# A gated-triangle mix stage in slots of four tiles instead of two, with fewer and wider norm chains

## The reference, cut to what matters

```
zn  = layernorm(layernorm(x)) * ln_g + ln_b               # x, and three pair inputs alike
ab  = sigmoid(zn @ Wg + bg) * (zn @ W + b)                # three gated projections, 64 channels
blk = einsum(pp, ab1) + einsum(ab2, lp) + ab3 * ip        # the triangle: 192 x 192 x 64
g   = sigmoid(zn @ Wend + bend)
x2  = x + g * (layernorm(blk) * lnc_g + lnc_b) @ Wsum ... * z_mask     # the mix stage
t   = layernorm(x2)
logits = mean over all positions of t, per channel, @ Wr + br          # routing: 2 of 8 experts
out = t-stream + ffn(t)                                                # the feed-forward stage
```

## Time and profile before

| | |
|---|---|
| median of three runs | 1568.2 us |
| the profiled execution's own time | 1569.81 us |
| its span | 1568.1 us |
| mean granted TensorE clock | 0.955 |
| busy share of the span | PE 88%, DVE 78%, POOL 64%, ACT 63% |
| DMA, mean over the span | 172 GB/s |

### The profile page before, as it was taken

One profiled execution on the slowest core, in us unless ns is written; L12 is line 12 of the kernel. 1 busy time (PEld: TensorE's weight loads), 2 busy tenths in 40 slices (PEclk: granted clock), 3 DMA queues, 4 the chain that ended last, 5 costly groups with the idle time before them and its releaser, 6 DMA issues. The chain is left out here.

```text
span 1568.1 us, 33771 instructions
## 1 busy us (share of the span) xinstructions
PE 1383.9 (88%) x9869; PEld 1152.2 (73%) x9869; DVE 1223.8 (78%) x4389; ACT 986.0 (63%) x2295; POOL 1007.0 (64%) x1547
## 2 busy tenths in 40 slices
PE   5999999999999996878778999779999999999992
PEld 2877777877777775767556666569898888999882
DVE  6898888888888973645479999757888888888874
ACT  3877777778778783322236777434676666766762
POOL 3888888888889884433337888533555555555553
PEclk9999999999999998989889999979999999999996
DMA  9989899989899978767678999311222222222212
GB/s 211 240 218 240 224 238 243 230 224 232 225 244 226 241 193 236 219 175 244 173 195 262 297 299 297 117 51 41 68 77 73 67 80 80 68 79 80 69 41 80
DMA packets 358354, 270.34 MB, mean 172 GB/s; under 512 B 60710, under 2 KB 333054, under 8 KB 358206
## 3 DMA queue, kind: packets, MB, share of 16 engines
q1 hardware_dynamic: 356924, 268.16, 63.7%
q10 hardware_dynamic: 1010, 0.20, 0.1%
q0 software_dynamic: 272, 0.21, 0.1%
HBM read 174.16 MB, written 94.37 MB: 171 GB/s over the span
## 5 line engine op out<-in xcount | busy, mean ns | idle before, releaser
L1466 ACT ACTIVATE hT<-psH_d,b 128x512 f32<-128x512 f32 x288 | 197.8, 689 | 171.4 <-PE psH_d L1506 171.3
L1491 PE MATMUL psY_d<-w,hT 128*128 128x128 f32 x2304 | 268.9, 275 | 0.0
L1491 PEld LDWEIGHTS psY_d<-w,hT 128*128 128x128 f32 x2304 | 262.9, 192 | 0.1
L639 PE MATMUL psZ_a<-w_all,xT_a 128*128 128x128 f32 x1728 | 239.1, 283 | 23.4 <-ACT xT_a L549 23.4
L639 PEld LDWEIGHTS psZ_a<-w_all,xT_a 128*128 128x128 f32 x1728 | 216.6, 197 | 30.8 <-ACT xT_a L549 28.4
L639 PE MATMUL psZ_a<-w_all,xT_block 128*128 128x384 f32 x576 | 213.3, 493 | 9.2 <-DVE ab_a L710 9.2
L565 ACT ACTIVATE sig_a<-psZ_a 128x256 f32<-128x256 f32 (+1 forms) x360 | 153.8, 427 | 93.3 <-PE psZ_a L639 53.5
L1524 POOL TENSOR_TENSOR u_d<-u_d,gamma 128x512 f32<-128x512 f32 x72 | 95.9, 1331 | 159.9 <-ACT u_d L1452 142.3
L626 PE MATMUL psT_a<-ident,shared 128*128 128x128 f32 x1152 | 189.3, 278 | 4.7 <-issue 3.3
L626 PEld LDWEIGHTS psT_a<-ident,shared 128*128 128x128 f32 x1152 | 143.8, 144 | 55.9 <-issue 28.0
L577 POOL TENSOR_SCALAR shared<-shared,coefs_ix 128x128 f32<-128x128 f32 x348 | 154.9, 456 | 39.6 <-DVE coefs_ix L360 37.4
(11 more groups left out here) (219 smaller groups left out, 3023.7 us busy)
## 6 DMA issues: line engine op xcount, KB each, us to landing
shared<-in_x_dram SPq DMA_DIRECT2D x48, 512.0 KB, 5.6
scratch_xT<-xT_block SPq DMA_DIRECT2D x36, 512.0 KB, 4.9
shared<-scratch_xT SPq DMA_DIRECT2D x36, 512.0 KB, 4.8
scratch_x<-x_c SPq DMA_DIRECT2D x36, 512.0 KB, 4.0
shared<-scratch_x SPq DMA_DIRECT2D x36, 512.0 KB, 3.6
shared<-in_x_dram SPq DMA_DIRECT2D x48, 256.0 KB, 5.1
shared<-L_conv_protein_pair_dram SPq DMA_DIRECT2D x24, 512.0 KB, 7.3
shared<-in_L_conv_l_pair_dram SPq DMA_DIRECT2D x24, 512.0 KB, 6.2
```

The costliest lines, as they stand in the source:

```text
L639: ins = nc.tensor.matmul(out, turned_x(G, i, t0, size)[:, j * P:j * P + P], rhs[i], start=True, stop=True)
L1466: nc.scalar.activation(hT[:, g % 2, f, :], psH[:, f, :], ACT.Gelu, bias=s["b1"][:, f:f + 1]).then_inc(gelued, 1)
L1491: ins = nc.tensor.matmul(psY[:, g % 2, i * CH:i * CH + CH], hT[:, g % 2, f, i * P:i * P + P], s["w2"][:, f, :], start=(f == 0), stop=(f == ...
```

## The change: what it does

- A slot is four tiles (a quad): 72 slots instead of 144 pairs. In a slot ACT normalises tiles 0 and 2 and POOL tiles 1 and 3, two slots ahead, into three buffers; PE makes two transposes, four psZ and two psW matmuls; the copy, gate, y and add work on 256, 512, 512 and 512 elements a row.
- Chains no longer follow the blocks. Ten chains (`CHAINS_C`): chains 0 to 2 for the triangle's quads 0 to 5, 6 to 11 and 12 to 20, chains 3 to 6 for 12, 12, 12 and 15 quads of the triangle together with 12 quads of x2 each, chains 7 to 9 for the last x2 quads. A chain has 18 steps; the last one makes the scale, shift and copy in up to three operations. Chains 1 and 2 have two slots (nine steps each), chains 3 to 8 three slots (six each), chain 0 and 9 stand alone. In a slot DVE interleaves: step, y, (triangle tiles); then four times step, one x2 tile, (triangle tiles); then any further steps.
- The triangle's tiles are measured ahead as `MEASURED` says: 12 a slot in slots 0 and 1, 6 in slots 2 to 7, 9 or 10 in 8 to 12, 4 in 13 to 36, 5 in 37 to 48, none after.
- x2 has three block buffers; route of a quad follows `ROUTED_IN`: one quad a slot from slot 17, two a slot from slot 65, three in 71 and 72, the last six after the last chain.
- `coef_t` is one buffer for all tiles, and x2's coefficients are used from the buffer that the FFN stage reads.

```diff
+QUADS = TPB // 4
+SLOTS_C = QUADS * NBLK
+X2_RING = 3
+TRI_GROUPS = ((0, 6), (6, 12), (12, 21), (21, 33), (33, 45), (45, 57), (57, 72))
+X2_GROUPS = ((0, 12), (12, 24), (24, 36), (36, 48), (48, 60), (60, 66), (66, 72))
+CHAINS_C = [(TRI_GROUPS[0], None), (TRI_GROUPS[1], None), (TRI_GROUPS[2], None), (TRI_GROUPS[3], X2_GROUPS[0]),
+            (TRI_GROUPS[4], X2_GROUPS[1]), (TRI_GROUPS[5], X2_GROUPS[2]), (TRI_GROUPS[6], X2_GROUPS[3]),
+            (None, X2_GROUPS[4]), (None, X2_GROUPS[5]), (None, X2_GROUPS[6])]
+MEASURED = [[] for _ in range(SLOTS_C)]
+for _c, _from, _to in ((1, 0, 2), (2, 2, 8), (3, 8, 13), (4, 13, 25), (5, 25, 37), (6, 37, 49)):
...
+CHAIN_STEPS_C = LN_STEPS + 1
+CHAIN_SLOTS = {1: (2, 2), 2: (8, 2), 3: (13, 3), 4: (25, 3), 5: (37, 3), 6: (49, 3), 7: (61, 3), 8: (67, 3), 9: (73, 1)}
...
+for _lo, _hi, _from, _per in ((0, 12, 17, 1), (12, 24, 29, 1), (24, 36, 41, 1), (36, 48, 53, 1), (48, 60, 65, 2), (60, 66, 71, 3),
+                              (66, 72, 73, 6)):
...
+        def norm_tri(wait, op, sem_out, Q, tiles):
+
+            c = TRI_CHAIN[Q]
+            if Q == CHAINS_C[c][0][0]:
+                wait(coefst_ready, 2 * tri_chains(c))
+            if Q > 2:
+                wait(turned, Q - 2)
...
         @block.scalar
...
+            for Q in range(SLOTS_C):
+                if Q + 2 < SLOTS_C:
+                    norm_tri(act.wait_ge, op, tri_normed_act, Q + 2, (0, 2))
+                if Q + 1 < SLOTS_C:
+                    copy_turned(Q + 1)
+                act.wait_ge(projected, Q + 1)
+                need(act, y_made, Q - 1)
+                nc.scalar.activation(gate[:, Q % 2], psZ[:, Q % 2, :].rearrange("p (t c) -> p t c", t=4),
                                      ACT.Sigmoid).then_inc(gated, 1)
...
         @block.gpsimd
...
+            for Q in range(SLOTS_C):
+                n, q = place(Q)
+                if Q + 2 < SLOTS_C:
+                    norm_tri(wait, op, tri_normed_pool, Q + 2, (1, 3))
+                k = q // 2
+                pool.wait_ge(y_made, Q + 1)
...
+                nc.gpsimd.tensor_tensor(x2[:, n % X2_RING, tiles, :], y[:, Q % 2], x_in[:, n % 2, tiles, :],
                                         ALU.add).then_inc(x2_made, 1)
...
         @block.tensor
...
+            for Q in range(LAST_C + 1):
+                if Q + 1 < SLOTS_C:
+                    turn(Q + 1)
...
+                    need(pe, gated, Q - 1)
+                    for i in range(4):
+                        ins = nc.tensor.matmul(psZ[:, Q % 2, CH * i:CH * i + CH], xT_in[:, n % 2, 4 * q + i, :], w_end,
                                                start=True, stop=True)
                     ins.then_inc(projected, 1)
+                    pe.wait_ge(copied, Q + 1)
+                    need(pe, y_made, Q - 1)
+                    for h in range(2):
+                        ins = nc.tensor.matmul(psW[:, Q % 2, 2 * CH * h:2 * CH * h + 2 * CH], triT[:, Q % 2, P * h:P * h + P], s["ws2"][:],
+                                               start=True, stop=True)
+                    ins.then_inc(tri_projected, 1)
+                for R in ROUTED_IN.get(Q, []):
+                    route(R)
...
         @block.vector
...
+            for Q in range(LAST_C + 1):
+                steps = STEPS_C.get(Q, [])
+                measured = MEASURED[Q] if Q < SLOTS_C else []
+                for part in range(max(5, len(steps))):
+                    if part < len(steps):
+                        coef_step(*steps[part])
+                    if part == 0 and Q < SLOTS_C:
+                        make_y(Q)
+                    if 1 <= part <= 4 and 1 <= Q <= SLOTS_C:
+                        stats_x2(Q - 1, part - 1)
+                    share = -(-len(measured) // 5)
+                    for t in measured[share * part:share * part + share]:
+                        stats_tri(t)
```

More of the change, by code:

```diff
@@ L123, in ln_step, with ln_mix_step @@
     ins.then_inc(stepped, 1)
[L126 to L130 removed]
+def ln_mix_step(nc, dve, step, stepped, before, stats, work, channels, coefs):
     v = nc.vector
[L136 to L141, removed]
+    lo, hi = channels[0][0], channels[-1][1]
+    mean2, m2, diff, sq, var, t = (work[:, q, lo:hi] for q in range(6))
+    y, shift = coefs[:, 0, lo:hi], coefs[:, 1, lo:hi]
+    of = stats[:, lo:hi]
     if step > 0:
@@ L942, in after, with place @@
[L942 to L960, removed]
+        def place(Q):
+            return Q // QUADS, Q % QUADS
@@ L962, in _, with tri_chains, x2_chains @@
+        def tri_chains(c):
+            return sum(tri is not None for tri, _ in CHAINS_C[:c + 1])
+        def x2_chains(c):
+            return sum(x2_group is not None for _, x2_group in CHAINS_C[:c + 1])
         @block.sync
         def _(sp):
[L966 to L977, removed]
@@ L996, in op, with copy_turned @@
                 return nc.scalar.activation(out, x, ACT.Identity, bias=b, scale=r)
[L998 to L1013, removed]
+            def copy_turned(Q):
+                act.wait_ge(turned, Q + 1)
+                need(act, tri_projected, Q - 1)
+                nc.scalar.copy(triT[:, Q % 2, :], psT[:, Q % 2, 0:2 * P]).then_inc(copied, 1)
+            for Q in range(2):
+                norm_tri(act.wait_ge, op, tri_normed_act, Q, (0, 2))
+            copy_turned(0)
+            for Q in range(SLOTS_C):
[6 more added lines that the diff above has]
+                nc.scalar.activation(gate[:, Q % 2], psZ[:, Q % 2, :].rearrange("p (t c) -> p t c", t=4),
                                      ACT.Sigmoid).then_inc(gated, 1)
[L1016 to L1019, removed]
         @block.gpsimd
@@ new lines, in make_y @@
+            def make_y(Q):
+                dve.wait_ge(tri_projected, Q + 1)
+                dve.wait_ge(gated, Q + 1)
+                need(dve, x2_made, Q - 1)
+                v.tensor_tensor(y[:, Q % 2], psW[:, Q % 2, :].rearrange("p (t c) -> p t c", t=4), gate[:, Q % 2],
+                                ALU.mult).then_inc(y_made, 1)
+            for t in range(4 * TRI_GROUPS[0][1]):
+                stats_tri(t)
+            for step in range(CHAIN_STEPS_C):
+                coef_step(0, step)
```

282 lines of the change are left out of this document (122 added, 160 removed).

## The result

The changed kernel takes 1590.8 us (median of 4 runs, 1588.24 to 1591.96), the one before 1566.9 on the same chip (4 runs, 1564.97 to 1568.58): a ratio of 1.0143, 95% interval 1.0128 to 1.0157. It is slower by 24 us where +22 was forecast. The profiled execution took 1590.85 us (span 1589.1, before 1568.1), so the traces have 21.0 us to account for.

A forecast was written before the change was run, and what follows sets the result against it. DVE was taken as the limit before the change. Mix y to y 213.4 against 195.2 (+18.2), start +2.5, tail +1.2: +21.9 on 1569.8 gives 1591.7, less 1.6 to the median: 1590 us, range 1570 to 1600.

The forecast's parts named there:

- first y later after the stage's start: Mix stage start: two groups of normalisations per engine and twice the matmuls come first; +2.5 us, bounds +1.5 and +3.5.
- slots 0 to 3: First two measure 12 tiles each, next two hold nine steps each, the last then awaits ACT: 2.2, 3.2, 4.6, 6.15 us.
- slots 8, 9: Chain 2 repeats the nine-step slots and ACT's coefficient wait, with 9 to 10 tiles measured: 5.1 and 6.7 us.
- slots 10 to 12: Mix slots behind chain 2, with 9 or 10 measurements each: 2.6+2.6+3.3, or 8.5 us.
- slots 61 to 70: End of the mix stage, with two short chains and double routes: 9.7+2.6+5.5+9.4+2.7, or 29.9 us.
- tail: After the last y: chain and six routes as before, but y, add and four measurements take 3.0 against 1.8: +1.2 us.
- POOL's loop: Plain slots: y, POOL's add and normalisations, PE's transpose, later y take 7.68 us for three slots, 2.56 each, without slack.
- rival (b): Chance 0.11: faster, 1562.6 us; DVE's relief alone counts, POOL's loop is shorter, slots 13 to 60 run at PE's 2.41.
- The collisions: Chain slots: a DVE step waits for POOL's add to end, 0.83 us beyond its cost, possibly 0 to 1.2.
- Rival (a): Chance 0.20: in chain slots the steps miss POOL's adds, so the same sum without those waits gives 1575.5 us.
- Rival (d): Chance 0.12: PE's clock falls more often in early slots, each further half-clock stretch costing up to 2.8 us: 1594 to 1600.
- What was counted as nothing: Three x2 buffers instead of two, ACT's longer instructions (about 1.7 a slot) and the SP queue were given no cost.

The follow-up runs named there:

- e1: The changed kernel with POOL normalising three slots ahead instead of two (four buffers of tri_n), ACT still two: 1576.8 us, ratio 1.006 to the kernel before.
- e2: The changed kernel with most of DVE's chain steps issued later, behind three x2 tiles with their triangle tiles: 1584.1 us, ratio 1.011 to the kernel before.
- e3: The changed kernel with both POOL three slots ahead and DVE's steps issued later: 1568.8 us, ratio 0.9996 to the kernel before.
- e7: The changed kernel with POOL three slots ahead, later steps, first chains joined, and 19 spare VectorE copies: 1561.5 us, ratio 0.9953 to the kernel before.

## Why the prediction was right

By its own steps, forecast against measured:

| term | forecast | measured |
|---|---|---|
| first y later after the stage's start | +2.5 | +2.5 |
| slots 0 to 3 | 2.2, 3.2, 4.6, 6.15 | 2.13, 3.02, 4.53, 6.11 |
| slots 4 to 7 | 11.1 | 11.4 |
| slots 8, 9 | 5.1, 6.7 | 5.13, 6.73 |
| slots 10 to 12 | 8.5 | 9.5 |
| slots 13 to 15 (chain) | 11.1 | 11.2 |
| slots 16 to 24 | 22.9 | 23.1 |
| slots 25 to 36 | 34.1 | 34.3 |
| slots 37 to 48, 49 to 60 | 34.5, 33.3 | 34.7, 33.5 |
| slots 61 to 70 | 29.9 | 28.4 |
| all, y to y | 213.4 | 213.7 |
| tail | +1.2 | +1.2 |

The sum is better than its terms: slots 10 to 12 were put 1.0 us too short and slots 61 to 70 1.5 too long (slot 64 by 0.5, slot 70 by 1.2), and the two errors nearly cancel.

**POOL's loop** was the step that carried the sign, and it held: 2.56 a slot forecast, 2.57 the mean of the plain ones (2.46 and 2.69 by turns). y to add was 0.78, add and normalisations 2.03, y to transpose 2.94 (3.03 forecast); e1 shows that POOL's lead holds PE there. But the loop was closed wrongly. The prediction put one PE slot between the transpose and the y and divided 7.68 by three; the trace closes it after two slots, 5.18 us, as the prediction's own condition for rival (b) had it (2x2.41-2.24). The slots that come as 2.46 and 2.69 by turns fit this: from slot 18 to 24 two neighbours always add up to 5.15 to 5.18, three to anything from 7.62 to 7.88. With the forecast's own terms two slots are 3.03 + 2.24 = 5.27, 2.64 a slot. That 2.56 came out so close is luck: a y to transpose 0.09 too long and a loop one slot too long work against each other. Its price, 14 us in time and 15.0 in the mix stretch, is one of two causes, about twice the other.

**The collisions** held in mechanism and, where e2 takes them away, in price. The long step, ended by the add, is in every chain slot. The four early slots (2, 3, 8, 9) were to gain 0.83 each without it, 3.3 in all; in e2 they are 0.78, 0.78, 0.92 and 0.91 shorter, 3.4. A later chain of three slots was to be 9.25 without and 11.1 with them; it is 11.2 with, and e2 has 10.0, 0.5 of which is the rest of the wait. So the bare slot was put 0.1 too low. The slots of e2 had a higher granted clock at 824 to 856 (0.89 against 0.79), so a part of the early 3.4 can be the clock's. Rival (a) priced all of them at 14.5 us (for "seven later chains"; six have slots); e2 shows 8.4, and what the remaining ones in the slots behind 48 cost was not measured.

**Rival (b)**, faster, was turned down for the right reason, a loop that lacks slack, and for a wrong one. The prediction held against it that a block would need 326 GB/s, above the 296 seen. The same 16 us in e1, e3 and e7:
```profile
872.00:888.00 16.00, 16.00 (x141) 12.05 (x140) 13.01 (x62) 10.49 (x27) 13.37 (x20) 1.00 0.99 315
```
```profile
872.00:888.00 16.00, 16.00 (x146) 11.75 (x145) 14.02 (x65) 10.90 (x27) 14.55 (x23) 1.00 1.04 327
```
```profile
872.00:888.00 16.00, 16.00 (x146) 11.75 (x145) 14.39 (x66) 10.95 (x27) 11.84 (x19) 1.00 1.08 338
```
The 296 of the earlier trace rows was what the kernel asked for, not what the queues give. Its time (1562.6) needs a shorter loop; with that loop opened and the collisions still there, e1 has 1576.8, and only e7, with the steps and the first chains changed as well, has 1561.5.

**Rival (d)**: the windows 824 to 840 and 840 to 856 both show a clock of 0.79 where before only the first did (the second was 1.00). PE idled 6.25 us ahead of slot 10. Slots 10 to 12, which follow, are the one early term that came out long, by 1.0 us. So the stretch came, and even if all of that 1.0 is the clock's, it cost about a third of the 2.8 allowed for.

**What was counted as nothing** stayed nothing: no wait for a buffer of x2 and none for SP is in the view. Not tried: the third buffer of x2 undone alone, and joint chains with slots of two tiles, so their shares of the remaining effects are not known.

On the port, the Trainium skill ("SBUF — State Buffer", "SBUF: two separate sides") has an instruction of GpSimd and one of VectorE with two inputs in SBUF exclude each other: the one that starts first holds the shared ports to its end. The adds bear it out (1.0 us steps, and e2 when they are moved away). The normalisations do not: in e7's slot the step at 885.91, with two operands from memory, took 0.25 us beside the two that began at 885.65, and in the kernel before 44 steps lie wholly inside one normalisation, none over 0.22 us.

## What to carry to other kernels

When slots are made wider, count every lead again in slots and in time: put down each in-order engine that serves two slots of different number, follow the loop that its first job closes through the other engines up to the first result that it releases, in each engine's order, and compare its sum with lead times slot. Before, 3.02 us stood against three pairs of 1.23; after, 5.18 against two slots of 2.46, and e1 gives it three. A loop without slack also never wins back lateness from elsewhere. Relief on the busiest engine pays only once that loop is open: the same change with one more buffer and another order of the same steps was level, and with joined first chains, and 19 idle copies that put a later loop back in its place, 0.5% faster. Before an edit is judged by the total, compare the stages whose code did not change.

## What the runs showed that was not expected

- Removing 19 instructions of VectorE ahead of a loop made the loop's stage 10 to 13 us slower (508.8 and 510.9 against 496 to 499 in the kernels that have them): two waits behind each jump back, 2.3 to 2.5 and 1.5 to 1.8 us, for which no semaphore is seen, and 15 more packets of instructions. Nineteen idle copies took them away; 45 in the changed kernel brought the first of the two, and 16 more packets.
- The collision lengthens whichever side comes second. The adds of 1.33 to 1.42 us in slots 13 to 39 are those that start while a step is still running for another 0.20 to 0.29 us; from slot 50 on, where at most 0.10 us of a step is left, an add takes 1.27 to 1.28 us although a step beside it takes 1.15 to 1.19.
- 338 GB/s at a DMA share of 1.08 (e7, 872 to 888 us): a share of 1.00 is no ceiling.
